# Layer-0 attention: one fused mask-and-minimum over both PSUM banks of a row, in place of a reduction, a fused operation and a combining minimum

## The reference, cut to what matters

```python
scores = jnp.einsum('bhqd,bhkd->bhqk', q, k) * HD ** (-0.5)
causal = jnp.tril(jnp.ones((T, T), bool))
scores = jnp.where(causal[None, None], scores, -jnp.inf)
attn = jax.nn.softmax(scores, axis=-1)
```

## Time and profile before

| | us |
|---|---|
| median of 3 runs | 1507.27 |
| lowest, highest | 1503.93, 1507.38 |
| the profiled execution | 1505.46 |
| its span, first to last instruction | 1503.7 |
| PE, DVE, ACT, POOL busy in it | 1383.7, 1103.2, 784.8, 280.3 |

### The profile page before, as it was taken

How to read it: one execution, slowest core, us unless ns; L and a number is a source line. 1 busy time by engine, 2 the same in 40 slices (tenths; PEclk the granted TensorE clock), 3 DMA queues, 4 the chain that set the end, 5 groups by cost and what they waited for, 6 DMA issues and landing times.

```text
span 1503.7 us, 27515 instructions
## 1 busy us (share of the span) xinstructions
PE 1383.7 (92%) x9204; PEld 1055.9 (70%) x9204; DVE 1103.2 (73%) x3389; ACT 784.8 (52%) x1701; POOL 280.3 (19%) x413
## 2 busy tenths in 40 slices
PE   4189999999999999889949999999999999989998
PEld 2167677777767776656627777788787777768887
DVE  3788888989888887452247778887878877855555
ACT  3315464555546555443327666666667666633322
POOL 4001011111101101000043323322222333400000
PEclk9589999999999999989979999999999999989999
DMA  2000000000000000300000000000000000000000
GB/s 96 0 2 1 1 1 1 2 1 1 1 1 2 1 2 1 137 5 0 0 14 1 1 2 1 1 2 1 1 1 2 1 2 1 1 1 1 0 0 28
DMA packets 5612, 12.02 MB, mean 8 GB/s; under 512 B 112, under 2 KB 5232, under 8 KB 5232
## 3 DMA queue, kind: packets, MB, share of 16 engines
q1 hardware_dynamic: 5488, 10.44, 1.9%
HBM read 9.39 MB, written 1.05 MB: 7 GB/s over the span
## 4 chain that ended last, share of the span: by engine, by line
PE 56%; DVE 4%; POOL 1%; ACT 1%; issue 1%; DVEq 0%; ACTq 0%; POOLq 0%
PE PS L2019 9%; PE PS L2033 8%; PE PS L2087 6%; PE PS L2012 5%; PE PS L2011 5%; PE PS L1960 5%; PE PS L2100 4%; PE PS L2046 4%; PE PS L2053 4%; PE PS L1980 2%; PE PS L2061 2%; PE PS L1656 2%; PE PS L1861 1%; PE PS L1878 1%; PE PS L1935 1%
## 5 line engine op out<-in xcount | busy, mean ns | idle before, releaser
L964 ACT ACTIVATE pe_<-PS 128x512 f32<-128x512 f32 (+3 forms) x384 | 176.0, 488 | 152.7 <-PE PS L1861 151.3
L1031 ACT ACTIVATE PN<-PS,NM 128x128 f32<-128x128 f32 (+7 forms) x256 | 189.7, 742 | 106.5 <-DVE NM L1529 52.3
L1529 DVE CUSTOM_DVE_ANT_0 PS<-PS,mask_row 128x128 f32<-128x128 f32 (+7 forms) x256 | 192.6, 773 | 41.9 <-PE PS L2012 38.2
L2011 PE MATMUL PS<-KA,QA 128*128 128x512 f32 (+3 forms) x384 | 161.5, 420 | 15.2 <-DVE KA L1568 14.4
L2019 PE MATMUL PS<-ident,PN 128*128 128x128 f32 x1152 | 170.8, 276 | 1.6 <-ACT PN L1031 1.5
L1841 PE MATMUL PS<-kta,qta 128*128 128x512 f32 (+3 forms) x384 | 146.0, 411 | 7.3 <-DVE tmqs L1340 2.4
L2019 PEld LDWEIGHTS PS<-ident,PN 128*128 128x128 f32 x1152 | 131.8, 141 | 27.7 <-issue 17.4
L1861 PE MATMUL PS<-qtb,kta 128*128 128x512 f32 (+3 forms) x384 | 136.3, 385 | 1.0 <-ACT pe_ L964 0.9
L2012 PE MATMUL PS<-KB,QA 128*128 128x512 f32 (+3 forms) x384 | 129.1, 348 | 0.0
L1340 DVE CUSTOM_DVE_ANT_0 PS<-PS,W 128x128 f32<-128x128 f32 (+3 forms) x256 | 124.7, 496 | 3.6 <-PE PS L1841 2.3
L786 POOL TENSOR_SCALAR_AFFINE_SELECT pe_<-pe_ 128x512 f32<-128x512 f32 x64 | 40.8, 637 | 407.2 <-ACT pe_ L964 407.2
(11 more groups left out here) (253 smaller groups left out, 3103.7 us busy)
## 6 DMA issues: line engine op xcount, KB each, us to landing
W<-w SPq DMA_DIRECT2D x1, 5124.0 KB, 15.8
W<-w SPq DMA_DIRECT2D x1, 2508.0 KB, 10.8
X<-x SPq DMA_DIRECT2D x2, 512.0 KB, 4.8
out<-X SPq DMA_DIRECT2D x1, 1024.0 KB, 5.1
WOZ<-w SPq DMA_DIRECT2D x2, 256.0 KB, 4.2
```

Source lines behind the costliest of these rows:

```text
L964: act.activation(pe_[:, h, n % 2, 0:w], PS[:, 4 + h % 2, 0:w], ACT.Exp, scale=HD0 ** -0.5)\
L1031: act.activation(prob_rows(u, r), scores_of(u), ACT.Exp, bias=NM[:, u:u + 1], scale=-1.0, accum_out=SM[:, r % 2, u:u + 1]).then_inc(score_ ...
L1529: dve.tensor_tensor_reduce(scores_of(u), scores_of(u), mask_row[:, S - w:S], -HD1 ** -0.5, -MASKED, ALU.add, ALU.min, NM[:, u:u + 1]).then ...
L2011: pe.matmul(piece, query, KA[:, b, h, lo:lo + n], start=True, stop=False)
```

## The change

For the later queries the two pieces of a row are still two matmuls into banks 2 and 3, but VectorE handles them in one fused instruction over both banks (640 to 1024 columns) once the second is there, and writes the row's result straight to its column of tmqs. The reduction, NMH0 and the combining minimum go. The mask grows from 512 to 1024 columns. PE's waits follow: a piece waits for the instruction that reads piece p - 2, which for an even piece is that of the whole row before.

```diff
-        mask_row0 = W1[:, 2 * HG * S:2 * HG * S + 512]
+        mask_row0 = W1[:, 2 * HG * S:2 * HG * S + 1024]
...
+        def read_by(p):
+
+            c, _, _, k = PIECES0[p]
+            return ("mx", p if k == c else p + 1)
...
                         c, h, i, k = PIECES0[r[1]]
+                        if k < c:
+                            continue
                         wait(dve, f0_pe, r, s)
...
-                        w = min(512, (i + 1) * P - 512 * k)
-                        piece = PS[:, 2 + r[1] % 2, 0:w]
-                        if k == c:
-                            dve.tensor_tensor_reduce(piece, piece, mask_row0[:, 512 - w:512], -1.0, -MASKED, ALU.add,
-                                                     ALU.min, dst).then_inc(f0_dve.sem, 1)
-                        else:
-                            dve.tensor_reduce(dst, piece, AX.X, ALU.max, negate=True).then_inc(f0_dve.sem, 1)
-                        if (c, i, k) == (1, TB - 1, 1):
-                            wait(dve, f0_dve, ("mx", r[1]), s)
-                            dve.tensor_tensor(tmq[:, 4:8, col], NMH0[:, h, :, 0], NMH0[:, h, :, 1], ALU.min)\
-                                .then_inc(f0_dve.sem, 1)
+                        n = (i + 1) * P
+                        row = PS[:, 2:4, :].rearrange("p k n -> p (k n)")[:, 512 * (1 - c) * (r[1] % 2):][:, 0:n]
+                        dve.tensor_tensor_reduce(row, row, mask_row0[:, 1024 - n:1024], -1.0, -MASKED, ALU.add, ALU.min,
+                                                 tmq[:, i, 32 * h + QM:32 * h + QM + 1]).then_inc(f0_dve.sem, 1)
...
-                            wait(pe, f0_dve, ("cb", HG - 1) if half else ("mx", P0_HALF - 1), s)
+                            wait(pe, f0_dve, ("mx", NP0 - 1) if half else ("mx", P0_HALF - 1), s)
...
                         if p >= 2:
-                            wait(pe, f0_dve, ("mx", p - 2), s)
+                            wait(pe, f0_dve, read_by(p - 2), s)
                         else:
-                            wait(pe, f0_dve, ("mx", NP0 - 2 + p), s, 1)
+                            wait(pe, f0_dve, read_by(NP0 - 2 + p), s, 1)
```

More of the change, by code:

```diff
@@ L110, in program @@
         ots = sb("ots", [P, 2, 512])
-        NMH0 = sb("NMH0", [P, HG, 4, 2])
         rz = sb("rz", [P, 2, 16])
@@ L133, in program @@
         W1 = sb("W1", [P, W1_N])
-        assert W1_N >= 2 * HG * S + 512
-        mask_row0 = W1[:, 2 * HG * S:2 * HG * S + 512]
+        assert W1_N >= 2 * HG * S + 1024
+        mask_row0 = W1[:, 2 * HG * S:2 * HG * S + 1024]
         with ExitStack() as early:
@@ L352, in vector_steps @@
                 elif r[0] == "a":
-                    vec.append(("mx", r[1]))
-                    c, h, i, k = PIECES0[r[1]]
-                    if (c, i, k) == (1, TB - 1, 1):
-                        vec.append(("cb", h))
+                    vec += [read_by(r[1])] if read_by(r[1])[1] == r[1] else []
                 elif r[0] == "pv" and r[1] in LAST:
@@ L707, in _ @@
             link(pool.memset(mask_row0, 0.0))
-            last = mask_row0[:, 512 - P:512]
+            last = mask_row0[:, 1024 - P:1024]
             link(pool.affine_select(out=last, in_=last, compare_op=ALU.is_ge, fill=MASKED, base=0,
@@ L1330, in slot @@
                         c, h, i, k = PIECES0[r[1]]
+                        if k < c:
+                            continue
                         wait(dve, f0_pe, r, s)
-                        col = 32 * h + QM
-                        if c == 0:
-                            dst = tmq[:, i, col:col + 1]
-                        else:
-                            dst = NMH0[:, h, i - 4, k:k + 1]
-                        w = min(512, (i + 1) * P - 512 * k)
-                        piece = PS[:, 2 + r[1] % 2, 0:w]
-                        if k == c:
-                            dve.tensor_tensor_reduce(piece, piece, mask_row0[:, 512 - w:512], -1.0, -MASKED, ALU.add,
-                                                     ALU.min, dst).then_inc(f0_dve.sem, 1)
-                        else:
-                            dve.tensor_reduce(dst, piece, AX.X, ALU.max, negate=True).then_inc(f0_dve.sem, 1)
-                        if (c, i, k) == (1, TB - 1, 1):
-                            wait(dve, f0_dve, ("mx", r[1]), s)
-                            dve.tensor_tensor(tmq[:, 4:8, col], NMH0[:, h, :, 0], NMH0[:, h, :, 1], ALU.min)\
-                                .then_inc(f0_dve.sem, 1)
+                        n = (i + 1) * P
+                        row = PS[:, 2:4, :].rearrange("p k n -> p (k n)")[:, 512 * (1 - c) * (r[1] % 2):][:, 0:n]
+                        dve.tensor_tensor_reduce(row, row, mask_row0[:, 1024 - n:1024], -1.0, -MASKED, ALU.add, ALU.min,
+                                                 tmq[:, i, 32 * h + QM:32 * h + QM + 1]).then_inc(f0_dve.sem, 1)
                     elif r[0] == "pv" and r[1] in LAST:
```

## The result

The changed kernel takes 1625.49 us (median of 4 runs, 1622.65 to 1628.02) against 1506.10 (1503.93 to 1507.38): 119.4 us slower, ratio 1.0792, 95% interval 1.0778 to 1.0805. The forecast was slower by 88.5, 1596 us, in a range up to 1614. The direction came as forecast, and so did the place of the loss. The size did not: it is 11.5 us beyond the range.

What follows compares the result with a forecast made beforehand. It took PE's queue as what delays the end, VectorE nearly full and 1.5 us behind at piece 23. 79 + 9 + 0.4 = 88.5 us on 1505.46 gives 1594, 1596 as median; range 1568 to 1614.

Steps and rivals of the forecast that it cites:

- seven slots with the clock at 1.00: Later slots of layer-0 attention: PE's waits for the row before add 11.3 us a slot, 79 us over seven.
- first slot: SLOT_HEAD, with fewer other products: a head goes from 6.9 to 9.2 us, 9 us in all.
- mask: Kernel start: VectorE's first instruction waits for GpSimd's memset of 512 more mask columns, 0.4 us.
- the walk: PE's and VectorE's queues carried together through one slot, giving PE's lateness at each boundary; 11.3 us a slot.
- each instruction at its old length: Rule for one slot: instructions keep their lengths and start at the latest of old neighbour and new wait.
- a fall of the clock: In slots: the forecast would be wrong if the granted clock fell from 1.00; no time was given for it.
- 7.25 us of lockstep: SLOT_HEAD: a head's four rows take 0.6 to 0.8 us each on PE and 0.89 to 1.29 on VectorE, 7.25 together.
- 2 of training: SLOT_HEAD: about 2 us of a head's training sweep finds no place beside its four rows.
- The eleven bare boundaries and the four covered ones: Fifteen row boundaries in a slot: at four the new wait is met already, at eleven PE stalls.
- VectorE's queue as the bound: Rival: VectorE's shorter work sets the pace, 16.6 us go, 1490 us; 3%.
- stalls taken up by old waits: Rival: PE's existing waits shrink, about half of eleven steps go, 6 us a slot, 1554 us; 10%.
- The third: Rival: training sweeps' handoffs show their whole latency, 5 us more a slot, 35 in all, 1631 us; 7%.

Runs made afterwards that it cites:

- fillers: Changed kernel with unread matmuls of 512 columns on PE ahead of the even pieces that wait; 1603.21 us, ratio 1.0651 to before.
- covered rows: Kernel before, with the fused two-bank instruction only for the five rows ending in pieces 33, 39, 43, 45, 47; 1511.20 us, ratio 1.0030.
- fused, one bank: Changed kernel, its fused instruction reading only 128 columns of the odd piece's bank repeatedly, even pieces written without a wait; 1512.48 us, ratio 1.0051.
- one combine: Kernel before with one combining minimum of 16 values at the end of a trip instead of four of 4; 1503.43 us, ratio 0.9981.
- wait alone: Kernel before, VectorE's work unchanged, only PE's even pieces waiting for the last instruction of the row before; 1567.83 us, ratio 1.0417.

## Why the prediction was wrong in its size

Point by point, by its own steps:

| term | predicted, us | measured, us |
|---|---|---|
| seven slots with the clock at 1.00 | 79 | 84.0 (7 x (78.90 - 66.90), fillers) |
| the clock in them | 0 | 20.7 |
| first slot | 9 | 13.9, of which 3.3 the clock |
| mask | 0.4 | 0.4 |
| sum | 88.5 | 119.0 |

**The step that failed** is the rule of the walk, "each instruction at its old length". PE's old lengths belong to a granted clock of 1.00, and that belonged to a PE that hardly stood. I named a fall of the clock as a sign that I was wrong, and gave it no price. The kernel before shows it at half where PE comes out of a long stand. From 56 to 69 us PE is busy 0.80 us, and the clock is 0.50 there and up to 76 us, in the first slot:

```profile
56.00:69.00 13.00, 0.80 (x2) 0.51 (x3) 9.10 (x5) 5.37 (x3) 1.22 (x4) 0.50 0.00 0
69.00:76.00 7.00, 5.71 (x23) 4.74 (x24) 4.37 (x15) 2.73 (x5) 1.56 (x7) 0.50 0.00 0
```

What the kernel before could not show is whether stalls as long as these bring it down inside a slot. After the change they are 1.56 and 1.97 us ahead of pieces 22 and 24, and it falls right behind them. Without the clock's some 24 us the time would be about 1601, inside the range. The Trainium skill ("TensorE: Matmul & The Clock Gate", section "HAM oscillation — how this bites in real kernels") describes a kernel that waits for transfers ahead of every tile and starts each at half clock again. The windows show the same kind of fall, 0.79 at two places in a slot, and 1.00 there with fillers, but here behind stalls of at most 1.97 us with work between them; the waits of that kernel are longer than these.

**The first slot** was mis-sized too. I had 7.25 us of lockstep and 2 of training a head. That is 9, and it measured 13.9. Its clock was 0.53; fillers brought it to 0.94 and 3.3 us back. At most 1.6 us more are left. Whether they lie in the lockstep or in the 2 us of training, and in which wait, stays open.

**The rest of the 5 us in slots** is small misses of the walk, 0.7 a slot. One I can point to is ahead of piece 24: 11.55 us from piece 18, where I had 10.94 (291.52 less 280.58). On its way to the row that releases it VectorE stands 0.23 us for a tanh (line 1244, at 250.92), and my walk had no such wait. The fillers themselves may account for some of it. In the working of the range, 1577 lacks the 1.8 us from that execution to the median (1505.46, 66.5, 5 and 1.8 are 1579); that changes nothing here.

**What held.** The eleven bare boundaries and the four covered ones: every stall of a slot stands ahead of a piece that the walk named, but for 0.19 us ahead of 46, and the covered rows alone cost 0.2 us a slot. Pieces 20 and 22 came within 0.1 us of their forecast distance from piece 18. The fused forms took their forecast time. The mask's memset is 0.4: VectorE's first instruction starts at 10.24, for 9.84:

```profile
10.24 0.87 DVE L1097 BATCH_NORM_STATS2 stats<-X 128x6 f32<-128x128 f32 x4 [10.24 <-POOL tmqs L728]
```

PE's waits for line 1338 are 96.8 us by the page, where I had 60 to 90, and VectorE's share of a slot is 71% (112.99 of 160 us from 300 to 460), for 88% before.

**The rivals.** The first, VectorE's queue as the bound, fell: with its work cut and PE nearly free (fused, one bank) the kernel is 0.5% slower than before. The queue is not without weight, as one combine shows. The 16.6 us of this rival also take 0.17 us for every minimum, where the one that closes a slot takes 0.52. The advice of the Trainium skill ("VectorE: DVE Perf Modes", section "Rules for kernel authors") to cut the number of instructions holds for what it counts: one minimum for four won 0.19%. It says nothing of what the fewer instructions hold while they run. The same row of that section also says not to fuse for speed, which the prediction left out, and here the fused kernel is the slower one; its reason there is another than the hold on the banks. The second, stalls taken up by old waits, fell: against the kernel before, PE is 0.7 us late at piece 18 of a slot and 15.2 at piece 46, and only the 0.3 that the walk had at the end comes back. The third had the right sign, and its 1631 lies near the measured time by luck. It priced handoffs at 35 us; the runs leave at most 5 us in slots and 1.6 in the first for them, and what cost more was the clock, which it did not name.

## What to carry to other kernels

- Two PSUM banks that one instruction reads are one buffer. Before fusing over both, count for each boundary the producer's other work until its next write, and compare it with the fused instruction, its accumulator read and two handoffs; or move the order so that this work stands there.
- When a walk through the trace finds repeated stalls of a microsecond or two on TensorE, allow for a fall of the clock: here some 24 of 119 us. It need not come (with the wait alone the clock in slots stayed at 1.00). Filling the stalls with work gave most or all of it back.
- A piece of VectorE's work that another engine waits on is judged by when it frees its buffer, not by its own length.

## What was not expected of the hardware

- Matmuls that nobody reads, put into PE's stalls, made the changed kernel 22 us faster, with 28 of them a slot.
- Stalls of at most 1.97 us, with work between them, brought the granted clock from 2.4 to 1.2 GHz twice a slot; in another kernel a stall of 1.46 us did not.
- The fused instruction takes 51 to 58 ns more when its initial value is read from memory and not given as a constant (702 to 753 ns for 512 columns, 300 to 356 for 128).
- The minimum of 4 values a partition takes 0.17 us in 25 of its 32 rows and 0.52 in the seven that begin 0.13 us behind GpSimd's mask instruction (line 786); these end within 0.02 us of it. The one of 16 values does the same: 0.19 us once, 0.53 or 0.54 in seven.
